# A low-rank factor taken tile by tile instead of two tiles at a time, in a decoder layer in fp32r

## The chip, the cores and the metric

The kernel runs on one core of a Trainium2 chip. The metric is the device time of one execution in microseconds. The kernel before took 524.78 us, the median of 3 runs (523.88 to 526.72).

## The reference, cut to what matters

One decoder layer on 8 sequences of 112 tokens, 1024 features each: self-attention with 16 heads, then cross-attention of each sequence to 375 context rows, then a linear layer with low-rank adapters. Each of the three is added to its input and normalised.

```python
x = layernorm(x + self_attn(x, Wq, Wk, Wv, Wo))     # x: 8 x 112 x 1024
x = layernorm(x + cross_attn(x, ctx))               # ctx: 8 x 375 x 1024
y = x @ weight.T + bias
A = lora_A[adapter_idx]; Bw = lora_B[adapter_idx]   # rank 16, 3 adapters, one per sequence
lo = (x @ A.T) @ Bw.T                               # "first factor", then "second factor"
x = layernorm(x + y + where(use_lora, lo, 0))
```

## The kernel before, in words

Tokens are tiles of 128: 8 x 112 = 896 tokens are 7 tiles. A tile crosses the border of two sequences, so a sequence is spread over at most two tiles. Every product is made in fp32r from a high and a low part of each operand: high by high, high by low and low by high, so three matmuls for each block of 128 features (`part`, L645 and on).

The last third of the kernel, from the end of the self-attention's output product, interleaves two streams on TensorE by a written order:

- the cross-attention of sequence b: `cross_score(b, ...)` (24 matmuls of 376 columns, cut in a first part of 18 and a last of 6), `turn_cprob(b, ...)` (3 transposes of the probabilities into the PSUM bank `CTURN`, bank 6), `cross_mix(b)` (18 matmuls of 512 columns), and `turn_row(b)` (8 transposes of the normalised rows, which give the linear layer its input `act_hi`, `act_lo`);
- the linear layer of tile i, output half n: `ffn(i, n)`, 24 matmuls of 512 columns (8 steps over k, three each), and then two more matmuls that add the adapters' second factor and the bias from `t_both` (`add_low`, L676 to L685).

`t_both` of a tile comes from the first factor. `low_rank` (L776 to L792) makes it for a pair of tiles: in the middle of `ffn(i, 0)` of the pair's second tile, after step k = 2, it issues 16 matmuls of 256 columns (tile 6 is alone: 128 columns) into bank 6, the same bank that `turn_cprob` uses. Then ScalarE copies the lower partitions out (`keep_t_part`, L1081) and VectorE adds them and multiplies by the selection of the adapter, with two writes for each of two segments per tile (`mask_t`, L1511). TensorE needs the result at `add_low`: that of the pair's first tile after step k = 6 of the same `ffn`, that of the second at its end.

So the first half-groups of a pair are finished together. The order on TensorE is: `ffn(0,0)`, `ffn(1,0)` with `low_rank`, `ffn(0,1)`, `ffn(1,1)`, `ffn(2,0)`, `ffn(3,0)` with `low_rank`, and so on, with the pieces of cross-attention between them.

Each engine works its queue in the written order and stops at a wait. ScalarE rounds loaded weights (`round_ff`, `round_cf`, `round_ct`), copies results out of PSUM (`keep_y`) and normalises (`norm_y`, `norm_x2`); VectorE makes the low parts (`rest_cf`, `rest_ct`, `rest_turned`) and statistics (`measure_y`, `add_row`); GpSimd makes the low parts of the linear layer's weights (`rest_ff`, L1757) and the reciprocal roots (`power`, L1741); SyncE issues the DMAs. `ffn` alternates between two PSUM banks, so `wait_bank` lets a group start when the one two before it has been copied out. `GROUPS` lists this order of groups; its index is what `group_done` and `y_kept` count. A ring of `T_RING` = 3 holds `t_both`.

In the functions below these waits matter: `low_rank` waits for `t_rest` (the previous pass has been used up by VectorE) and for `cprob_rest` (the probabilities in bank 6 have been read); `turn_cprob` waits for `t_rest` with its argument `low`.

Of the kernel before, what the change touches and what calls it, by code (L numbers as in the profile page):

```python
# [7 lines left out]
F32 = mybir.dt.float32  # L8
F32R = mybir.dt.float32r
I32 = mybir.dt.int32  # L10
ALU = mybir.AluOpType
# [37 lines left out]
          + [(i, n) for j in range(0, TILES, 2) for n in range(2) for i in range(j, min(j + 2, TILES))])  # L49
# [43 lines left out]


def pair_of(j):

    return range(2 * j, min(2 * j + 2, TILES))


def pair_cols(j):  # L100
    return slice(2 * j * P, min(2 * j + 2, TILES) * P)
# [6 lines left out]
def tile_of(i):  # L108
    return slice(i * P, i * P + P)
# [13 lines left out]
def build(nc, x_feat, x_tok, qkv_w, wo_w, ffn_w, ctx_feat, ctx_tok, starts, rotary, causal,  # L123
          identity, route, out):
    st = ExitStack()
    with st:
        def at(name, shape, where, dt=F32):
            return nc.alloc_sbuf_tensor_at(name, shape, dt, offset=BASE + where)
# [59 lines left out]
        ctop = at("ctop", [S, B, 4], S0 + 32544)  # L188
# [31 lines left out]
        t_part = small("t_part", [RA, 2 * P])  # L220
# [3 lines left out]
        norm = [small("norm1", [P, TILES, 6]), small("norm2", [S, B, 6]), small("norm3", [P, TILES, 6])]  # L224
        assert spot[0] <= 212832, spot
# [87 lines left out]
        def _(sp):  # L313
# [164 lines left out]
            load_cf(19)  # L478
            load_ff(9)
            load_cf(20)  # L480
# [52 lines left out]
        def _(pe):  # L533
# [143 lines left out]
            def add_low(i, n):  # L677

                to = GROUP[group_of(i, n, 1)]
                pe.wait_ge(b_rest, 1)  # L680
                pe.wait_ge(t_rest, 2 * i + 2)
                pe.matmul(to[:, :], t_both[:, i % T_RING, :], b_hi[:, 4 * n:4 * n + 4, :],  # L682
                          start=False, stop=False)
                pe.matmul(to[:, :], t_both[:, i % T_RING, :], b_lo[:, 4 * n:4 * n + 4, :],  # L684
                          start=False, stop=True).then_inc(group_done, 1)  # L685
# [90 lines left out]
            def low_rank(j, turns):  # L776

                cols = pair_cols(j)
                w = cols.stop - cols.start
                pe.wait_ge(a_rest, 1)  # L780
                pe.wait_ge(cprob_rest, turns)
                if j:
                    pe.wait_ge(t_rest, 4 * j)
                for k in range(KT):
                    if k == 0:
                        pe.matmul(CTURN[0:SECOND + RA, 0:w], a_both[:, k, :], act_hi[:, k, cols],
                                  start=True, stop=False)
                    pe.matmul(CTURN[0:SECOND, 0:w], a_both[:, k, 0:SECOND],
                              act_lo[:, k, cols], start=False, stop=False)
                    if k > 0:  # L790
                        last = pe.matmul(CTURN[0:SECOND + RA, 0:w], a_both[:, k, :],
                                         act_hi[:, k, cols], start=False, stop=(k == KT - 1))  # L792
                last.then_inc(t_done, 1)
# [75 lines left out]
            ffn(0, 0)  # L869
# [39 lines left out]
        def _(act):  # L909
# [171 lines left out]
            def keep_t_part(j):  # L1081
                w = P * len(pair_of(j))
                act.wait_ge(t_done, j + 1)
                if j:
                    act.wait_ge(t_added, j)
                act.activation(t_part[:, 0:w], CTURN[SECOND:SECOND + RA, 0:w],
                               ACT.Copy).then_inc(t_part_kept, 1)
# [95 lines left out]
            round_cf(19)  # L1183
            round_ff(9)
            round_cf(20)
            round_cf(21)
            round_ff(10)
            norm_x1(6)
            round_ct(23)
            round_ff(11)  # L1190
            cross_exp(4)
            round_ff(12)
# [9 lines left out]
            round_ct(26)  # L1202
            round_ct(27)
            keep_y(0, 0)
            round_ct(28)
            keep_cprob_t(4)
# [21 lines left out]
            norm_y(1)  # L1228
            round_cf(28)
            round_cf(29)  # L1230
            round_ct(35)
# [3 lines left out]
            keep_t_part(1)  # L1235
            norm_x2(5)
            round_ct(37)
            round_ct(38)
            keep_y(2, 0)
            round_ct(39)  # L1240
            round_ct(40)
            keep_cprob_t(6)
            keep_y(3, 0)
# [5 lines left out]
            norm_y(2)  # L1249
# [19 lines left out]
            norm_y(5)  # L1269
            keep_t_part(3)  # L1270
# [8 lines left out]
        def _(dve):  # L1279
# [231 lines left out]
            def mask_t(j):  # L1511


                w = P * len(pair_of(j))
                dve.wait_ge(t_part_kept, j + 1)
                dve.tensor_tensor(CTURN[0:RA, 0:w], CTURN[0:RA, 0:w], t_part[:, 0:w],
                                  ALU.add).then_inc(t_added, 1)
                dve.wait_ge(low_set, 2)
                dve.wait_ge(t_added, j + 1)
                for i in pair_of(j):  # L1520
                    if i >= T_RING:
                        dve.wait_ge(group_done, group_of(i - T_RING, 1, 1) + 1)
                    at_i = P * (i % 2)
                    for b, _, r, n in segments(i):
                        dve.tensor_scalar(t_both[0:RA, i % T_RING, r:r + n],
                                          CTURN[0:RA, at_i + r:at_i + r + n],
                                          sel[:, b:b + 1], None, ALU.mult).then_inc(t_rounded, 1)
                    for m, (b, _, r, n) in enumerate(segments(i)):
                        dve.wait_ge(t_rounded, 2 * i + m + 1)
                        dve.scalar_tensor_tensor(out=t_both[SECOND:SECOND + RA, i % T_RING, r:r + n],  # L1530
                                                 in0=CTURN[0:RA, at_i + r:at_i + r + n],
                                                 scalar=sel[:, b:b + 1],
                                                 in1=t_both[0:RA, i % T_RING, r:r + n].bitcast(F32),
                                                 op0=ALU.mult, op1=ALU.subtract).then_inc(t_rest, 1)
# [85 lines left out]
            rest_ct(18)  # L1620
            rest_ct(19)
            rest_cprob_t(3)
# [4 lines left out]
            add_wo(13)  # L1627
            rest_cf(19)
# [3 lines left out]
            rest_ct(23)  # L1632
            add_row(3)
            rest_turned("a5")
            rest_cf(22)
            mask_t(0)
            rest_ct(24)
            rest_ct(25)
            rest_ct(26)
            rest_cprob_t(4)  # L1640
            rest_ct(27)
            rest_ct(28)
            measure_y(0, 0)
# [19 lines left out]
            rest_cf(27)  # L1663
            rest_cf(28)
            rest_cf(29)
            cross_top(6)
# [3 lines left out]
            mask_t(1)  # L1670
            rest_ct(36)
            rest_ct(37)
            rest_ct(38)
            rest_ct(39)
            rest_cprob_t(6)
            rest_ct(40)
            measure_y(2, 0)
            measure_y(3, 0)
            rest_turned("b5")
            rest_cf(31)  # L1680
            measure_y(2, 1)
# [8 lines left out]
            rest_ct(46)  # L1690
            measure_y(3, 1)
            rest_turned("b6")
            rest_ct(47)
            add_row(7)
            mask_t(2)
            measure_y(4, 0)
            measure_y(5, 0)
            measure_y(4, 1)
            rest_turned("b7")
            measure_y(5, 1)  # L1700
            mask_t(3)
# [9 lines left out]
        def _(pool):  # L1711
# [90 lines left out]
            rest_ff(8)  # L1802
            rest_ff(9)
            power(0, 6, P)
# [85 lines left out]
```

## Time and profile before

| | |
|---|---|
| median of 3 runs | 524.78 us (523.88 to 526.72) |
| the profiled execution | 525.95 us, of which the span from first to last instruction is 524.2 us |
| TensorE matmuls | busy 515.3 us, 98% of the span, 2868 instructions |
| VectorE / ScalarE / GpSimd | busy 320.3 us (61%) / 261.7 us (50%) / 152.2 us (29%) |
| chain that ended last | TensorE 97%, VectorE 2% |
| granted TensorE clock | 0.997 of full speed, mean over the span |

The page gives the busy time of each engine and, in "the chain that ended last", what each stretch of the span hung on, followed back from the last instruction. A matmul's own duration in the rows (0.39 us for 512 columns) overlaps with its neighbours; what it costs the stream is the distance from its start to the next start. The profiled execution's time is the span and 1.75 us around it.

### The profile page before, as it was taken

What the parts mean: (1) busy time and instruction counts of PE and PEld (TensorE: products, weight loads), DVE (VectorE), ACT (ScalarE), POOL (GpSimd) and SP (SyncE); (2) the same over time, 40 slices, a digit from 0 to 9 for tenths busy, and PEclk for the clock granted to TensorE, in tenths of its full rate; (3) what the DMA queues carried; (4) which work ended last, traced back from release to release, by engine and by line L of the source; (5) the groups of instructions that cost most, each with busy time, mean ns of one, the idle gap of its engine ahead of it and who ended that gap; (6) DMA issues with size and microseconds to landing.
All of it is one profiled execution on the core that took longest, in us unless ns stands there. A gap on an engine that the chain in (4) does not pass through costs nothing.

```text
span 524.2 us, 7773 instructions
## 1 busy us (share of the span) xinstructions
PE 515.3 (98%) x2868; PEld 444.7 (85%) x2868; DVE 320.3 (61%) x660; ACT 261.7 (50%) x663; POOL 152.2 (29%) x139
## 2 busy tenths in 40 slices
PE   8999999999999999999999999999998999999995
PEld 5888888999999999999978888888887888988884
DVE  4832000177776868677674797779987776845432
ACT  5713210173846648384565356357777464525231
POOL 0003600436353554642006250114946010110010
PEclk9999999999999999999999999999999999999998
DMA  9906712331112111100087577579986466433011
GB/s 285 314 16 167 195 40 81 107 136 41 41 48 75 42 40 43 41 1 1 1 257 183 138 207 211 148 198 265 274 243 193 126 194 225 109 87 111 2 75 47
DMA packets 37958, 65.60 MB, mean 125 GB/s; under 512 B 4872, under 2 KB 20616, under 8 KB 37920
## 3 DMA queue, kind: packets, MB, share of 16 engines
q1 hardware_dynamic: 37392, 64.84, 42.9%
q8 instruction: 23, 0.38, 0.3%
q10 hardware_dynamic: 528, 0.26, 0.2%
q14 instruction: 15, 0.12, 0.1%
HBM read 54.08 MB, written 3.67 MB: 110 GB/s over the span
## 4 chain that ended last, share of the span: by engine, by line
PE 97%; DVE 2%; issue 0%; ACT 0%; POOL 0%; POOLq 0%; DVEq 0%
PE bank L536 30%; PE bank L651 29%; PE bank L547 15%; PE bank L737 6%; PE bank L563 3%; PE bank L578 3%; PE bank L770 2%; PE bank L768 2%; PE bank L773 2%; PE bank L721 1%; PE bank L609 1%; PE bank L710 1%; PE bank L682 1%; PE bank L684 1%; DVE cf_lo L1506 1%; PE bank L752 0%
## 5 line engine op out<-in xcount | busy, mean ns | idle before, releaser
L536 PE MATMUL bank<-x_hi,w_hi 128*128 128x448 f32 x256 | 94.3, 368 | 0.0
L536 PE MATMUL bank<-x_hi,w_lo 128*128 128x448 f32 x256 | 93.5, 365 | 0.0
L536 PE MATMUL bank<-x_lo,w_hi 128*128 128x448 f32 x256 | 93.5, 365 | 0.0
L1359 DVE STREAM_TRANSPOSE prob_t<-prob 32x256 f32<-32x256 f32 x160 | 69.7, 436 | 13.0 <-ACT prob L942 10.3
L651 PE MATMUL bank<-wo,act_hi 128*128 128x512 f32 x224 | 70.2, 395 | 0.0
L651 PE MATMUL bank<-ffn,act_hi 128*128 128x512 f32 x224 | 69.9, 393 | 0.0
L1728 POOL TENSOR_TENSOR w_lo<-w_mix,w_hi 128x1024 fp32r<-128x1024 f32 x16 | 38.2, 2389 | 105.2 <-ACT w_hi L917 105.2
L932 ACT ACTIVATE prob<-prob,shift 112x112 f32<-112x112 f32 x128 | 47.8, 375 | 38.9 <-DVE shift L1342 38.9
L1741 POOL TENSOR_TENSOR norm<-norm,minus_half 128x1 f32<-128x1 f32 (+1 forms) x22 | 16.6, 754 | 159.9 <-DVE norm L1432 159.9
L536 PEld LDWEIGHTS bank<-x_hi,w_hi 128*128 128x128 f32 x256 | 48.1, 188 | 4.7
L536 PEld LDWEIGHTS bank<-x_hi,w_lo 128*128 128x128 f32 x256 | 48.1, 188 | 3.8
L536 PEld LDWEIGHTS bank<-x_lo,w_hi 128*128 128x128 f32 x256 | 48.1, 188 | 3.7
L651 PEld LDWEIGHTS bank<-wo,act_hi 128*128 128x128 f32 x224 | 41.3, 188 | 8.7
L651 PEld LDWEIGHTS bank<-ffn,act_hi 128*128 128x128 f32 x224 | 41.2, 188 | 8.1
L1028 ACT ACTIVATE ct_hi<-ct_raw 125x512 fp32r<-125x512 f32 x48 | 28.8, 625 | 33.2 <-DMA ct_raw<-ctx_tok 19.8
L917 ACT ACTIVATE w_hi<-w_mix 128x1024 fp32r<-128x1024 f32 x16 | 16.9, 1054 | 54.8 <-PE bank L536 47.0
L651 PE MATMUL bank<-wo,act_lo 128*128 128x512 f32 x112 | 43.7, 390 | 0.0
L651 PE MATMUL bank<-ffn,act_lo 128*128 128x512 f32 x112 | 43.7, 390 | 0.0
L1506 DVE TENSOR_TENSOR cf_lo<-cf_raw,cf_hi 128x752 fp32r<-128x752 f32 x32 | 34.3, 1081 | 7.8 <-ACT cf_hi L1016 7.6
L942 ACT ACTIVATE prob<-prob,inv 112x112 f32<-112x112 f32 x128 | 37.3, 375 | 0.1
L1322 DVE TENSOR_TENSOR q_feat<-bank,turn 128x448 f32<-128x448 f32 x16 | 9.9, 619 | 43.4 <-PE bank L536 43.3
L1499 DVE TENSOR_TENSOR ct_lo<-ct_raw,ct_hi 125x512 fp32r<-125x512 f32 x48 | 32.9, 719 | 5.4 <-ACT ct_hi L1028 5.1
(114 smaller groups left out, 984.1 us busy)
## 6 DMA issues: line engine op xcount, KB each, us to landing
cf_raw<-ctx_feat SPq DMA_DIRECT2D x32, 376.0 KB, 4.3
ct_raw<-ctx_tok SPq DMA_DIRECT2D x24, 448.0 KB
w_raw<-qkv_w SPq DMA_DIRECT2D x16, 512.0 KB, 3.4
half_raw<-wo_w SPq DMA_DIRECT2D x16, 256.0 KB, 6.0
half_raw<-ffn_w SPq DMA_DIRECT2D x16, 256.0 KB, 6.1
wv_raw<-qkv_w SPq DMA_DIRECT2D x15, 256.0 KB, 7.5
x_raw<-x_feat SPq DMA_DIRECT2D x7, 448.0 KB, 8.2
out<-y_t SPq DMA_DIRECT2D x6, 512.0 KB, 3.6
```

Of the source, the lines that this page charges most:

```text
L536: last = pe.matmul(to[:, 0:HT], a[:, k, :], b[:, k, HT * h:HT * h + HT], start=(k == 0 and b is x_hi and a is w_hi[w]), stop=(k == KT - 1 ...
L547: return pe.matmul(value_bank(c, i)[:, :], a[:, k, tile_of(i)], w[c][:, k, :], start=(k == 0 and a is x_hi and w is wv_hi), stop=(k == KT ...
L651: last = pe.matmul(to[:, :], a[:, k, cols], weight(of, n, k, w), start=(k == 0 and a is act_hi and w == 0), stop=(ends and k == KT - 1 and ...
L737: last = pe.matmul(CSCORE[0:S, 0:LKP], a[:, k, tokens_of(b)], c[slot][:, kk, :], start=(k == 0 and a is act_hi and c is cf_hi), stop=(k == ...
L917: act.activation(w_hi[w][:, :, :], w_mix[:, :, :], ACT.Copy).then_inc(w_rounded, 1)
L932: last = act.activation(prob[a][:, b, :], prob[a][:, b, :], ACT.Exp, bias=shift[:, a, b:b + 1], accum_out=total[:, a, b:b + 1])
L942: last = act.activation(prob[a][:, b, :], prob[a][:, b, :], ACT.Copy, scale=inv[:, a, b:b + 1])
L1028: act.activation(ct_hi[m % CT_HI][:, :], ct_raw[c][:, HALF * n:HALF * n + HALF], ACT.Copy).then_inc(ct_rounded, 1)
L1359: return dve.transpose(quads(prob_t_wide[r], key, query), quads(prob_wide[r], query, key))
L1499: dve.tensor_tensor(ct_lo[c][:, cols], ct_raw[c][:, cols], ct_hi[m % CT_HI][:, :].bitcast(F32), ALU.subtract).then_inc(ct_rest[n], 1)
L1506: dve.tensor_tensor(cf_lo[slot][:, :, :], cf_raw[slot][:, :, :], cf_hi[slot][:, :, :].bitcast(F32), ALU.subtract).then_inc(cf_rest, 1)
L1728: pool.tensor_tensor(w_lo[w][:, :, :], w_mix[:, :, :], w_hi[w][:, :, :].bitcast(F32), ALU.subtract).then_inc(w_rest, 1)
```

## The change

The first factor is made for one tile at a time: `low_rank(i)` issues its 16 matmuls with 128 columns after step k = 2 of every `ffn(i, 0)`, and each half-group is finished by its own two `add_low` matmuls at its end. The four passes (three of 256 columns and one of 128) become seven of 128. `GROUPS` for tiles 2 to 6 becomes (2,0), (2,1), (3,0), (3,1), ...; tiles 0 and 1 keep (0,0), (1,0), (0,1), (1,1). `keep_t_part` and `mask_t` follow it, seven in place of four; `t_part` is half as wide, and `ctop` gets a place of its own. The queues of ScalarE, VectorE, GpSimd and SyncE are written anew around this from the fifth sequence's scores on.

```diff
 GROUPS = (...
-          + [(i, n) for j in range(0, TILES, 2) for n in range(2) for i in range(j, min(j + 2, TILES))])
+          + [(0, 0), (1, 0), (0, 1), (1, 1)]
+          + [(i, n) for i in range(2, TILES) for n in range(2)])
@@ sync
             load_ff(8)
             load_cf(19)
+            load_cf(20)
             load_ff(9)
-            load_cf(20)
...
             load_cf(31)
+            store_y(2)
             load_ct(7, 0)
             load_ct(7, 1)
             load_ct(7, 2)
-            store_y(2)
@@ tensor
             def ffn(i, n, turns=0):
                 ...
                 for k in range(KT):
                     part(1, i, n, k, GROUP[g], ends=False)
-                    if n == 0 and k == 2 and i == pair_of(i // 2)[-1]:
-                        low_rank(i // 2, turns)
-                    if n == 0 and k == 6 and i % 2:
-                        add_low(i - 1, 0)
-                if n or i == pair_of(i // 2)[-1]:
-                    add_low(i, n)
+                    if n == 0 and k == 2:
+                        low_rank(i, turns)
+                pe.wait_ge(b_rest, 1)
+                pe.wait_ge(t_rest, 2 * i + 2)
+                pe.matmul(GROUP[g][:, :], t_both[:, i % T_RING, :], b_hi[...], ...)
+                pe.matmul(GROUP[g][:, :], t_both[:, i % T_RING, :], b_lo[...], ...).then_inc(group_done, 1)
...
-            def low_rank(j, turns):
-                cols = pair_cols(j)
-                w = cols.stop - cols.start
+            def low_rank(i, turns):
+                cols = tile_of(i)
                 pe.wait_ge(a_rest, 1)
+                pe.wait_ge(turn_rest, 2 * AT_TURN[f"b{i + 1}"] + 2)
                 pe.wait_ge(cprob_rest, turns)
-                if j:
-                    pe.wait_ge(t_rest, 4 * j)
+                if i:
+                    pe.wait_ge(t_rest, 2 * i)
                 # the same 16 matmuls, over P columns in place of w
...
-            ffn(0, 0)
+            ffn(0, 0, 4)
...
-            ffn(2, 0)
+            ffn(2, 0, 6)
             cross_score(6, last)
             cross_mix(5)
-            ffn(3, 0, 6)
-            turn_cprob(6, 4)
+            ffn(2, 1)
+            turn_cprob(6, 3)
             cross_score(7, first)
             turn_row(5)
-            ffn(2, 1)
+            ffn(3, 0, 7)
             cross_score(7, last)
             cross_mix(6)
             ffn(3, 1)
             turn_cprob(7, 4)
-            ffn(4, 0)
+            ffn(4, 0, 8)
             turn_row(6)
             cross_mix(7)
+            ffn(4, 1)
             ffn(5, 0, 8)
-            ffn(4, 1)
             turn_row(7)
             ffn(5, 1)
@@ scalar (the places of keep_t_part and keep_y; the rest moves by one or two)
             round_cf(19)
+            keep_t_part(0)
+            round_cf(20)
             round_ff(9)
...
             norm_x1(6)
+            keep_y(0, 0)
             round_ct(23)
...
             round_ff(15)
+            keep_t_part(1)
+            norm_x2(3)
             round_ct(24)
-            keep_t_part(0)
-            norm_x2(3)
...
             norm_y(1)
+            keep_t_part(2)
...
             round_turned("b5")
             round_cf(31)
-            keep_y(2, 1)
+            keep_t_part(3)
+            norm_y(2)
+            keep_y(3, 0)
...
             round_ct(46)
             keep_y(3, 1)
+            keep_t_part(4)
+            keep_y(4, 0)
             round_turned("b6")
             round_ct(47)
             norm_y(3)
-            keep_t_part(2)
             norm_x2(7)
-            keep_y(4, 0)
+            keep_y(4, 1)
+            norm_y(4)
+            keep_t_part(5)
             keep_y(5, 0)
-            keep_y(4, 1)
             round_turned("b7")
-            norm_y(4)
@@ vector (mask_t's places)
             add_wo(13)
+            mask_t(0)
             rest_cf(19)
...
             rest_turned("a5")
+            mask_t(1)
             rest_cf(22)
-            mask_t(0)
...
             rest_cf(27)
+            mask_t(2)
...
             rest_cf(31)
+            mask_t(3)
             measure_y(3, 0)
...
             rest_ct(46)
+            mask_t(4)
             measure_y(3, 1)
...
             measure_y(4, 1)
+            mask_t(5)
             measure_y(5, 0)
@@ gpsimd
             rest_ff(8)
+            power(0, 6, P)
             rest_ff(9)
-            power(0, 6, P)
```

## Rows read from the trace of the kernel before

**Rows 1.** The page: busy time, granted clock in 40 slices, chain that ended last.

```profile
PE 515.3 (98%) x2868; PEld 444.7 (85%) x2868; DVE 320.3 (61%) x660; ACT 261.7 (50%) x663; POOL 152.2 (29%) x139
...
PEclk9999999999999999999999999999999999999998
...
PE 97%; DVE 2%; issue 0%; ACT 0%; POOL 0%; POOLq 0%; DVEq 0%
```

**Rows 2.** Waits of TensorE, 300 us to the end: who, for whom, us, times, longest.

```profile
PE bank L682 <- DVE t_both L1530: 1.5, 1, 1.5
```

**Rows 3.** TensorE in time order, first pair's pass: start, us, line, idle before.

```profile
398.97 0.28 PE L786 MATMUL bank<-act_hi,a_both 128*112 128x256 f32 x1
...
400.85 0.63 PE L651 MATMUL bank<-ffn,act_hi 128*128 128x512 f32 x2
...
402.90 0.62 PE L651 MATMUL bank<-ffn,act_hi 128*128 128x512 f32 x2
...
405.26 0.47 PE L682 MATMUL bank<-b_hi,t_both 128*128 128x512 f32 x1 [1.52 <-DVE t_both L1530]
405.57 0.39 PE L684 MATMUL bank<-b_lo,t_both 128*128 128x512 f32 x1
```

**Rows 4.** VectorE and GpSimd in time order, around that wait.

```profile
399.39 1.28 DVE L1455 TENSOR_TENSOR act_lo<-bank,act_hi 128x512 fp32r<-128x512 f32 x2
400.58 3.12 DVE L1506 TENSOR_TENSOR cf_lo<-cf_raw,cf_hi 128x752 fp32r<-128x752 f32 x1
...
404.65 0.47 DVE L1530 SCALAR_TENSOR_TENSOR t_both<-bank,sel,t_both 48x112 fp32r<-48x112 f32 x2
...
400.36 2.54 POOL L1757 TENSOR_TENSOR ffn<-half_raw,ffn 128x512 fp32r<-128x512 f32 x2
```

**Rows 5.** Line 1506 alone: ns min/median/max of its 32 instructions.

```profile
L1506 DVE TENSOR_TENSOR cf_lo<-cf_raw,cf_hi x32: 927/942/3118, 303.9 to 457.9; 128x752 fp32r<-128x752 f32 x32
```

**Rows 6.** TensorE, the third pair's pass.

```profile
486.11 0.28 PE L786 MATMUL bank<-act_hi,a_both 128*112 128x256 f32 x1
...
487.97 0.62 PE L651 MATMUL bank<-ffn,act_hi 128*128 128x512 f32 x2
```

**Rows 7.** TensorE, the pass of tile 6, 128 columns, and the adding matmul.

```profile
506.95 0.22 PE L786 MATMUL bank<-act_hi,a_both 128*112 128x128 f32 x1
...
508.17 0.68 PE L651 MATMUL bank<-ffn,act_hi 128*128 128x512 f32 x2
...
511.65 0.39 PE L682 MATMUL bank<-b_hi,t_both 128*128 128x512 f32 x1
```

**Rows 8.** ScalarE and VectorE behind the passes of pair 3 and tile 6.

```profile
488.17 0.38 ACT L1086 ACTIVATE t_part<-bank 48x256 f32<-48x256 f32 x1 [5.55 <-PE bank L791]
...
509.13 0.27 ACT L1086 ACTIVATE t_part<-bank 48x128 f32<-48x128 f32 x1
...
510.32 0.47 DVE L1530 SCALAR_TENSOR_TENSOR t_both<-bank,sel,t_both 48x16 fp32r<-48x16 f32 x2
```

**Rows 9.** TensorE, ScalarE and VectorE where tile 0's pass will come.

```profile
385.28 0.71 PE L651 MATMUL bank<-ffn,act_hi 128*128 128x512 f32 x2
...
386.55 0.84 ACT L1016 ACTIVATE cf_hi<-cf_raw 128x752 fp32r<-128x752 f32 x1
...
388.63 3.39 DVE L1506 TENSOR_TENSOR cf_lo<-cf_raw,cf_hi 128x752 fp32r<-128x752 f32 x3
```

**Rows 10.** ScalarE, TensorE, VectorE where tiles 2, 4 and 5 will come.

```profile
435.01 1.25 ACT L1103 ACTIVATE y_t<-y_t,norm 128x1024 f32<-128x1024 f32 x1 [0.28 <-POOL norm L1744]
...
473.59 0.71 PE L651 MATMUL bank<-ffn,act_hi 128*128 128x512 f32 x2
...
474.73 0.50 DVE L1490 TENSOR_TENSOR cprob_lo<-bank,cprob_hi 125x336 fp32r<-125x336 f32 x1
...
498.19 0.93 PE L721 MATMUL bank<-ident,row 112*128 112x112 f32 x8
...
501.13 1.24 ACT L1103 ACTIVATE y_t<-y_t,norm 128x1024 f32<-128x1024 f32 x1 [1.28 <-POOL norm L1744]
```

More of the change, by code:

```diff
@@ L92, in copies_of @@
     return [(b, n) for b in range(B) for n, piece in enumerate(pieces(b)) if piece[0] == i]
[L95 to L101, printed above, removed]
 def tokens_of(b):
@@ L675, in wo @@
                 last.then_inc(group_done, 1)
[L677 to L685, printed above, removed]
             def ffn(i, n, turns=0):
@@ L694, in ffn @@
                     part(1, i, n, k, GROUP[g], ends=False)
-                    if n == 0 and k == 2 and i == pair_of(i // 2)[-1]:
-                        low_rank(i // 2, turns)
-                    if n == 0 and k == 6 and i % 2:
-                        add_low(i - 1, 0)
-                if n or i == pair_of(i // 2)[-1]:
-                    add_low(i, n)
+                    if n == 0 and k == 2:
+                        low_rank(i, turns)
+                pe.wait_ge(b_rest, 1)
+                pe.wait_ge(t_rest, 2 * i + 2)
+                pe.matmul(GROUP[g][:, :], t_both[:, i % T_RING, :], b_hi[:, 4 * n:4 * n + 4, :],
+                          start=False, stop=False)
+                pe.matmul(GROUP[g][:, :], t_both[:, i % T_RING, :], b_lo[:, 4 * n:4 * n + 4, :],
+                          start=False, stop=True).then_inc(group_done, 1)
             def turn_tile(i):
@@ L774, in cross_mix @@
                                   start=False, stop=(c == CC - 1)).then_inc(ct_used, 1)
-            def low_rank(j, turns):
-                cols = pair_cols(j)
-                w = cols.stop - cols.start
+            def low_rank(i, turns):
+                cols = tile_of(i)
                 pe.wait_ge(a_rest, 1)
+                pe.wait_ge(turn_rest, 2 * AT_TURN[f"b{i + 1}"] + 2)
                 pe.wait_ge(cprob_rest, turns)
-                if j:
-                    pe.wait_ge(t_rest, 4 * j)
+                if i:
+                    pe.wait_ge(t_rest, 2 * i)
                 for k in range(KT):
                     if k == 0:
-                        pe.matmul(CTURN[0:SECOND + RA, 0:w], a_both[:, k, :], act_hi[:, k, cols],
+                        pe.matmul(CTURN[0:SECOND + RA, 0:P], a_both[:, k, :], act_hi[:, k, cols],
                                   start=True, stop=False)
-                    pe.matmul(CTURN[0:SECOND, 0:w], a_both[:, k, 0:SECOND],
+                    pe.matmul(CTURN[0:SECOND, 0:P], a_both[:, k, 0:SECOND],
                               act_lo[:, k, cols], start=False, stop=False)
                     if k > 0:
-                        last = pe.matmul(CTURN[0:SECOND + RA, 0:w], a_both[:, k, :],
-                                         act_hi[:, k, cols], start=False, stop=(k == KT - 1))
+                        last = pe.matmul(CTURN[0:SECOND + RA, 0:P], a_both[:, k, :],
+                                         act_hi[:, k, cols],
+                                         start=False, stop=(k == KT - 1))
                 last.then_inc(t_done, 1)
@@ L1079, in round_low, with keep_t_part @@
                 act.activation(b_hi[:, :, :], b_raw[:, :, :], ACT.Copy).then_inc(b_rounded, 1)
[L1081 to L1086, printed above, removed]
+            def keep_t_part(i):
+                act.wait_ge(t_done, i + 1)
+                if i:
+                    act.wait_ge(t_added, i)
+                act.activation(t_part[:, :], CTURN[SECOND:SECOND + RA, 0:P],
                                ACT.Copy).then_inc(t_part_kept, 1)
@@ L1234, in _ @@
             round_ct(36)
-            keep_t_part(1)
             norm_x2(5)
             round_ct(37)
+            keep_cprob_t(6)
             round_ct(38)
-            keep_y(2, 0)
             round_ct(39)
             round_ct(40)
-            keep_cprob_t(6)
-            keep_y(3, 0)
+            keep_y(2, 1)
             round_turned("b5")
             round_cf(31)
-            keep_y(2, 1)
+            keep_t_part(3)
+            norm_y(2)
+            keep_y(3, 0)
             round_ct(41)
             cross_exp(7)
-            norm_y(2)
             round_ct(42)
@@ L1260, in _ @@
             norm_y(3)
-            keep_t_part(2)
             norm_x2(7)
-            keep_y(4, 0)
+            keep_y(4, 1)
+            norm_y(4)
+            keep_t_part(5)
             keep_y(5, 0)
-            keep_y(4, 1)
             round_turned("b7")
-            norm_y(4)
             keep_y(5, 1)
             norm_y(5)
-            keep_t_part(3)
+            keep_t_part(6)
             keep_y(6, 0)
@@ L1508, in rest_cf, with mask_t @@
                                   ALU.subtract).then_inc(cf_rest, 1)
[L1511 to L1516, printed above, removed]
+            def mask_t(i):
+                dve.wait_ge(t_part_kept, i + 1)
+                dve.tensor_tensor(CTURN[0:RA, 0:P], CTURN[0:RA, 0:P], t_part[:, :],
                                   ALU.add).then_inc(t_added, 1)
@@ L1518, in mask_t @@
                 dve.wait_ge(low_set, 2)
[L1519 to L1534, printed above, removed]
+                if i >= T_RING:
+                    dve.wait_ge(group_done, group_of(i - T_RING, 1, 1) + 1)
@@ new lines, in mask_t @@
+                dve.wait_ge(t_added, i + 1)
+                for b, _, r, n in segments(i):
+                    dve.tensor_scalar(t_both[0:RA, i % T_RING, r:r + n], CTURN[0:RA, r:r + n],
+                                      sel[:, b:b + 1], None, ALU.mult).then_inc(t_rounded, 1)
+                for m, (b, _, r, n) in enumerate(segments(i)):
+                    dve.wait_ge(t_rounded, 2 * i + m + 1)
+                    dve.scalar_tensor_tensor(out=t_both[SECOND:SECOND + RA, i % T_RING, r:r + n],
+                                             in0=CTURN[0:RA, r:r + n], scalar=sel[:, b:b + 1],
+                                             in1=t_both[0:RA, i % T_RING, r:r + n].bitcast(F32),
+                                             op0=ALU.mult, op1=ALU.subtract).then_inc(t_rest, 1)
@@ L1620, in _ @@
             rest_ct(18)
+            rest_cprob_t(3)
             rest_ct(19)
-            rest_cprob_t(3)
             rest_ct(20)
@@ L1669, in _ @@
             rest_cf(30)
-            mask_t(1)
             rest_ct(36)
             rest_ct(37)
+            rest_cprob_t(6)
             rest_ct(38)
             rest_ct(39)
-            rest_cprob_t(6)
             rest_ct(40)
-            measure_y(2, 0)
+            rest_turned("b5")
+            measure_y(2, 1)
+            rest_cf(31)
+            mask_t(3)
             measure_y(3, 0)
-            rest_turned("b5")
-            rest_cf(31)
-            measure_y(2, 1)
             cross_top(7)
@@ L1694, in _ @@
             add_row(7)
-            mask_t(2)
-            measure_y(4, 0)
+            measure_y(4, 1)
+            mask_t(5)
             measure_y(5, 0)
-            measure_y(4, 1)
             rest_turned("b7")
             measure_y(5, 1)
-            mask_t(3)
+            mask_t(6)
             measure_y(6, 0)
```

17 lines of the change are left out of this document (9 added, 8 removed).

## The prediction

> **What bounds the kernel now.** I read the page's busy times, its clock row and its chain first. TensorE's matmuls fill 98% of the span, its clock is at the higher of its two levels in every slice but a last one, and 97% of the chain that ended last is TensorE [rows 1]. So the time is the length of TensorE's stream plus the holes in it. Next come TensorE's waits: over the last 224 us there is one, for `t_both`, 1.5 us [rows 2]. Every other engine's work is under cover there. I therefore price two things, the length of what TensorE issues and the holes, and for the reordered queues I only ask whether they open a hole. Last I read TensorE in time order around the passes of `low_rank`, and the other engines beside the hole.
>
> **The passes get dearer.** A pass of 256 columns takes 400.85 - 398.97 = 1.88 us, and the third 487.97 - 486.11 = 1.86 [rows 3, 6]; the second shows the same, so 1.87 each, 117 ns for each of 16 matmuls. A pass of 128 columns takes 508.17 - 506.95 = 1.22 us, 76 ns each [rows 7]: half the columns cost 65%. A step over k of `ffn` is (402.90 - 400.85) / 3 = 0.683 us [rows 3]; behind the pass of 128 columns, five steps take 511.65 - 508.17 = 3.48 in place of 3.42, so I charge that pass 0.06 more: 1.28. Tile 6 has its pass already. Three pairs' passes go, 3 x 1.87 = 5.61, and six single ones come, 6 x 1.28 = 7.68: **+2.07 us**, all on TensorE and thus on the path, +0.69 for each pair. Bounds: if a single pass costs half of a pair's (0.94), the sum is +0.03; if it is charged the 117 ns of the wide matmul, 1.87 each, it is +5.6. I take the row of the same instruction with the same columns, 1.28, which is the nearest there could be.
>
> The Trainium skill bears on this ("TensorE: Matmul & The Clock Gate", Back-to-back issue gap): it gives an isolated matmul of 128 columns about 56 ns. By that a pass would be 0.9 us and the passes no dearer than before; the row's 76 ns speaks against it. The same section's figure for a stream with weight loads, about 81 ns, is close to the row.
>
> The other instructions on TensorE stay: 14 pairs of adding matmuls, the same `ffn` matmuls, the same transposes, with the same kinds of neighbours. Splitting the passes also doubles `keep_t_part` and `mask_t` on ScalarE and VectorE; they have idle time, priced below as slack.
>
> **The hole closes.** `add_low(0,0)` could have started at 402.90 + 0.68 = 403.58 and started at 405.26, and the next matmul came 0.31 behind it where the usual distance is 0.23: the hole costs 1.68 + 0.08 = **1.76 us** [rows 3]. Its cause: `mask_t(0)` stands on VectorE behind `rest_cf(22)`, which took 3.12 us (median of its line 0.94) because GpSimd ran two `rest_ff` at 400.36 to 402.90 [rows 4, 5]. In the new order `mask_t(0)` runs 14 us earlier, and `mask_t(1)` stands ahead of `rest_cf(22)`. I take the whole 1.76 as gone. If it stayed, the sum is dearer by 1.76; more than this hole cannot be gained, since there is no other.
>
> What stalled can be read in the trace: an instruction with both inputs in SBUF beside GpSimd's reading ones; the subtraction of `act_lo`, one input in PSUM, kept its usual 0.64 us each until 400.58 [rows 4]. The Trainium skill says the same as a rule ("SBUF — State Buffer", Who interferes with whom): such a pair blocks, a VectorE instruction with at most one SBUF input does not. `mask_t`'s reads are of that kind, so by the rule `mask_t(1)` would pass GpSimd's last two `rest_ff`, which now come at the same time; if the rule failed there, a wait of up to 1 us returns.
>
> **Is a new hole opened?** After its own pass a tile's `t_both` is now needed five steps later, 3.48 us [rows 7]. At the least it takes 0.20 us until ScalarE starts (488.17 - 487.97) and 510.32 + 0.47 - 509.13 = 1.66 from there to the last write [rows 6, 8]: 1.86, which leaves 1.6 us for whatever is ahead in the two queues.
> - Tile 0: pass at 385.28 + 2.14 = 387.42 to 388.64 [rows 9]. ScalarE has finished `round_cf(19)` at 387.4 and VectorE `add_wo(13)` at 388.6 [rows 9]: slack 1.6. Behind `mask_t(0)` waits `rest_cf(19)`, done about 391.5; `cross_score(4, last)` needs it at 392.6. GpSimd's `rest_ff(9)` can hold it 1.2 us longer: 0 to 0.2 us of wait.
> - Tile 1: TensorE is 1.28 + 0.46 = 1.74 late here, pass ends about 401.9; VectorE is through `rest_turned(a5)` at 400.58 + 1.74 = 402.3 [rows 4], so `t_both` comes about 404.0 against a need at 405.4: slack 1.4.
> - Tile 2: `norm_y(1)` is ahead on ScalarE and ended at 436.26 [rows 10]; the pass will end about 435.5, so ScalarE is up to 0.8 late: slack 0.9. Tile 3 has `rest_cf(31)` ahead on VectorE, which follows the same `turn_row` as the pass does: about the same.
> - Tile 4: ahead are the last three `round_ct` and `rest_ct`, done about when the pass ends: slack about 1.2. This pass has a new wait of its own: bank 6 must be free of the probabilities of sequence 7. They were read at 474.73 + 0.50 = 475.23, and the pass would be reached at 473.59 + 2.15 = 475.74 [rows 10]: slack 0.5, the thinnest. What waits behind it on TensorE is everything.
> - Tile 5: `norm_y(4)` is ahead. It starts 501.13 - 498.19 = 2.94 after its group's end and takes 1.24 [rows 10], 4.2 in all; the pass ends 2.1 + 1.2 = 3.3 after it. So ScalarE is 0.9 late and the slack 0.7 to 0.9.
>
> None reaches zero. SyncE's two moves (`load_cf(20)` before `load_ff(9)`, `store_y(2)` before three loads) and `power(0, 6)` before `rest_ff(9)` on GpSimd: what they overtake is needed many us later (`store_y(2)` waits for `norm_y(2)`, which ScalarE now does before `cross_mix(6)` starts, and the loads wait for that product anyway). Zero, with 0 to 0.5 as bounds. The bank waits (`y_kept`) follow the group two before, which ended over 6 us earlier. The tail after the last product is untouched.
>
> **Sum.** +2.07 - 1.76 = +0.3 us. On the profiled execution's own terms the span goes 524.2 to 524.5 and its time 525.95 to 526.3. The median of the runs, 524.78, is 1.2 below the profiled execution; I put the difference on it: **525.1 us**.
>
> **The rivals.**
> - *One hole is left or a new one of its size comes* (the slack of 0.5 at tile 4, `rest_cf(19)` at tile 0): +2.07 - 1.76 + 1.7 = +2.0, 526.8. For it: four places under 1 us. Against: the work ahead in the queues shifts with TensorE itself.
> - *The hole was that execution's own.* The profiled one is 1.2 slower than the median, and the hole comes of GpSimd taking its turn 0.2 us before VectorE. If the timed runs have none, the change only costs: 526.9. Against: that turn follows from VectorE's own statistics, in each run alike.
> - *The other side: `t_both` late at every tile.* Each group now ends on its own pass, with nothing of the other tile between. The first pair's chain took 405.12 - 400.85 = 4.3 us from the pass [rows 3, 4]. If each of six new passes has such a chain, each costs 4.3 - 3.48 + 0.2 = 1.0, and with no hole gone elsewhere: +2.07 - 1.76 + 6.0 = +6.3, 531.1. It decides from a chain of 3.48 us on. Two of before speak against it: tile 6's was done at 510.79, 2.6 us after its pass, though ScalarE came 0.96 late to it, and pair 3's ScalarE started 0.2 behind its pass [rows 6 to 8].
> - *Cheap passes.* At half the pair's price the sum is +0.03 - 1.76 = -1.7, 523.1.
> - *The change doesn't do what it says:* no sign, the passes are plainly seven.
>
> **Chances.** Forecast 60%; a hole left or new 14%; the hole not in the timed runs 12%; late at every tile, in part or whole, 8%; cheap passes 6%. A measurement of this kernel tells about 0.5% from no change, 2.6 us, so only the chain late at most tiles is slower by more, with a little of the two middle cases, and hardly anything is faster. Faster 3%, same 87%, slower 10%. Range 523.1 to 527.5: from cheap passes to a new hole with some delay beside it; above lies the rest of the late chains. The forecast's own range is 524.3 to 526.1.
>
> **What would show it.** Seven passes of some 1.2 us, none of 256 columns; no wait at L682's counterpart, or one of tenths; the span's matmul count up by 48; `rest_cf(22)` may still be long, behind `mask_t(1)`. From the last `turn_row` to the end TensorE's order is the same, so the shift must be complete there: +0.3. The step from the first pair alone should be 2 x 1.28 - 1.87 - 1.76 = -1.1, then +0.7 for each of two pairs. I am wrong if waits for `t_both` or for bank 6 appear, or if single passes cost other than 1.2 to 1.35.

## The result, and the profile after

The changed kernel took 526.49 us, the median of 22 runs (525.85 to 527.56), against 525.07 us for the kernel before in 22 runs (523.69 to 526.72). The ratio is 1.0029, 95% interval 1.0021 to 1.0037: slower by 1.1 to 1.9 us. The two medians lie 1.42 apart, the ratio says +1.5. Forecast were +0.3 us and 525.1 us. The time lies in the stated range (523.1 to 527.5), but outside the forecast's own (524.3 to 526.1), and the shift is several times the forecast's.

The page of the changed kernel, its lines on busy time, granted clock and the chain that ended last, as in [rows 1]:

```profile
PE 516.7 (98%) x2916; PEld 446.8 (85%) x2916; DVE 318.5 (61%) x663; ACT 262.2 (50%) x666; POOL 152.0 (29%) x139
...
PEclk9999999999999999999999999999999999999999
...
PE 98%; ACT 1%; DVE 0%; issue 0%; POOL 0%; POOLq 0%; ACTq 0%
```

TensorE has 48 matmuls more, as counted, and bounds the kernel as before. Its waits from 300 us on (who, for whom, us, times, longest) answer to [rows 2]:

```profile
PE bank L751 <- DVE ct_lo L1485: 0.6, 1, 0.6
```

The wait for `t_both` is gone and another has come. TensorE in time order shows where: `turn_row(2)`, the pass of tile 0 and what follows it, its adding matmul, the wait inside `cross_mix(3)`, `turn_cprob(4)`, and `turn_row(7)`.

```profile
383.90 0.93 PE L704 MATMUL bank<-ident,row 112*128 112x112 f32 x8
...
386.74 0.22 PE L769 MATMUL bank<-act_hi,a_both 128*112 128x128 f32 x1
...
387.96 0.68 PE L643 MATMUL bank<-ffn,act_hi 128*128 128x512 f32 x2
...
391.44 0.39 PE L680 MATMUL bank<-b_hi,t_both 128*128 128x512 f32 x1
...
396.17 0.39 PE L756 MATMUL bank<-ct_hi,cprob_lo 125*112 125x512 f32 x1
397.14 0.49 PE L751 MATMUL bank<-ct_hi,cprob_hi 125*112 125x512 f32 x1 [0.58 <-DVE ct_lo L1485]
...
406.03 0.48 PE L735 MATMUL bank<-ident,cprob 112*125 112x112 f32 x3
...
498.73 0.45 PE L704 MATMUL bank<-ident,row 112*128 112x112 f32 x3
```

The pass takes 387.96 - 386.74 = 1.22 us, as read from tile 6 [rows 7]. The wait costs 397.14 - 396.17 - 0.23 = 0.74 us, and about 0.1 behind it.

The two spans, 524.2 and 524.7, differ by 0.5 only, and that is misleading. `turn_row(2)`, ahead of everything that the change touches, starts at 383.90 here and at 384.58 before. The lead is there already at the first query projection (first start in the window, the last column but one: 82.9 us before, 82.2 after):

```profile
L528 PE MATMUL bank<-x_hi,w_hi x30: 362/366/370, 82.2 to 99.8; 128*128 128x448 f32 x30
```

So I compare stretches between fixed marks of TensorE's stream, in us. The stretch "first" goes from `turn_row(2)` to `turn_cprob(4)` and holds the first two passes and both places of waits; "middle" goes on to `turn_row(7)`; "end" to the end of the span.

| execution | `turn_row(2)` starts | first | middle | end |
|---|---|---|---|---|
| before, shown above | 384.58 | 22.37 | 91.24 | 26.0 |
| before, e9 / e10 / e11 | 385.00 / 385.22 / 385.23 | 21.26 / 20.67 / 21.40 | 91.24 / 91.24 / 91.22 | 26.0 each |
| changed, shown here | 383.90 | 22.13 | 92.70 | 26.0 |
| changed, e1 / e12 | 385.05 / 384.94 | 21.33 / 21.63 | 92.69 / 92.72 | 25.9 / 26.0 |
| e3, e4, e5 (before, altered) | 385.08 / 385.33 / 384.85 | 21.54 / 20.59 / 20.82 | 91.22 / 91.24 / 91.21 | 26.0 / 25.9 / 26.0 |
| e2, e6 (changed, altered) | 384.95 / 384.31 | 21.50 / 21.50 | 92.72 / 92.72 | 25.9 / 26.0 |

Middle and end repeat within 0.1 us; the start varies by 1.4 us and "first" by 1.8. The middle is 1.46 longer in the changed kernel, for two pairs of tiles. In what follows, the loss of an execution in "first" is what it takes over the shortest of its kind: 20.59 in e4 for the kernel before, 21.33 in e1 for the changed one, the two with no stop of TensorE in their traces.

### The profile page after: what moved, and what is told of

It is laid out like the page before. It is cut to its first block, busy times and chain, and to the rows that moved or that the text cites. A ratio compares the mean times of both kernels' runs of the same rounds, so it can differ in the third digit from the quotient of the medians.

```text
span 524.7 us, 7890 instructions
## 1 busy us (share of the span) xinstructions
PE 516.7 (98%) x2916; PEld 446.8 (85%) x2916; DVE 318.5 (61%) x663; ACT 262.2 (50%) x666; POOL 152.0 (29%) x139
## 4 chain that ended last, share of the span: by engine, by line
PE 98%; ACT 1%; DVE 0%; issue 0%; POOL 0%; POOLq 0%; ACTq 0%
PE bank L528 30%; PE bank L643 29%; PE bank L539 15%; PE bank L720 6%; PE bank L555 3%; PE bank L570 3%; PE bank L751 2%; PE bank L753 2%; PE bank L756 2%; PE bank L704 1%; PE bank L693 1%; PE bank L774 1%; PE bank L601 1%; PE bank L771 1%; PE bank L682 1%; PE bank L680 1%
## 5 line engine op out<-in xcount | busy, mean ns | idle before, releaser
L1012 ACT ACTIVATE ct_hi<-ct_raw 125x512 fp32r<-125x512 f32 x48 | 28.5, 623 | 35.0 <-DMA ct_raw<-ctx_tok 23.0
L539 PE MATMUL bank<-wv_hi,x_hi 128*128 128x512 f32 x112 | 36.2, 393 | 0.0
```

Of the source, the lines that this page charges most:

```text
L539: return pe.matmul(value_bank(c, i)[:, :], a[:, k, tile_of(i)], w[c][:, k, :], start=(k == 0 and a is x_hi and w is wv_hi), stop=(k == KT ...
L1012: act.activation(ct_hi[m % CT_HI][:, :], ct_raw[c][:, HALF * n:HALF * n + HALF], ACT.Copy).then_inc(ct_rounded, 1)
```

## The experiments

**e1: the changed kernel again.** No edit.

> The changed kernel unaltered, for comparison on the same chip. Theory: in the stretch that the change touches (from the start of ffn(0,0)) TensorE's passes cost +2.07 us, the old hole of 1.76 is gone, and a new hole of 0.8 us stands in cross_mix(3), where its last chunk of context waits for its low part: sum +1.1 to +1.4 against the kernel before, ratio about 1.0025, with the new hole in the trace at the same place. Rival (the old hole was not in the timed runs of before): the ratio is above that, 1.0045 or so, since the gain of 1.76 would be missing.

Measured: 527.16 us against 525.35, ratio 1.0038 (1.0022 to 1.0054), that is +2.0 us (1.2 to 2.8), between the theory and the rival. The wait in `cross_mix(3)` is not there in its trace. ScalarE in time order shows why the place is shaky: two roundings of weights, one of context features and `round_ct(23)` (L1012):

```profile
390.87 0.63 ACT L1054 ACTIVATE ffn<-half_raw 128x512 fp32r<-128x512 f32 x1 [0.56 <-DMA half_raw<-ffn_w]
392.50 0.83 ACT L1000 ACTIVATE cf_hi<-cf_raw 128x752 fp32r<-128x752 f32 x1 [0.99 <-DMA cf_raw<-ctx_feat]
393.64 0.63 ACT L1054 ACTIVATE ffn<-half_raw 128x512 fp32r<-128x512 f32 x1 [0.31 <-DMA half_raw<-ffn_w]
...
395.93 0.62 ACT L1012 ACTIVATE ct_hi<-ct_raw 125x512 fp32r<-125x512 f32 x1
```

The same of the first profile of the changed kernel, with `norm_x1(6)` (L1017) and `keep_y(0,0)` (L1081):

```profile
390.61 0.63 ACT L1054 ACTIVATE ffn<-half_raw 128x512 fp32r<-128x512 f32 x1 [1.45 <-DMA half_raw<-ffn_w]
392.20 0.84 ACT L1000 ACTIVATE cf_hi<-cf_raw 128x752 fp32r<-128x752 f32 x1 [0.96 <-DMA cf_raw<-ctx_feat]
393.36 0.63 ACT L1054 ACTIVATE ffn<-half_raw 128x512 fp32r<-128x512 f32 x1 [0.33 <-DMA half_raw<-ffn_w]
393.90 1.23 ACT L1017 ACTIVATE x_t<-x_t,norm 128x1024 f32<-128x1024 f32 x1
395.15 0.60 ACT L1081 ACTIVATE y_t<-bank 128x512 f32<-128x512 f32 x1
395.65 0.62 ACT L1012 ACTIVATE ct_hi<-ct_raw 125x512 fp32r<-125x512 f32 x1
```

TensorE is 1.15 us later in e1 (385.05 against 383.90), but the loads land only 0.28 later (393.64 against 393.36). ScalarE takes them in order, so `round_ct(23)` follows the loads' clock, and TensorE waits for it if it is early. In this stretch the DMA engines are full; the last three numbers of this row of the changed kernel's windows (granted clock, DMA share, GB/s) say so:

```profile
390.00:395.00 5.00, 5.00 (x25) 4.12 (x24) 4.90 (x9) 3.11 (x4) 2.60 (x4) 1.00 1.04 263
```

Between these two executions a lead from the kernel's start is partly handed back here.

**e2: the changed kernel, SyncE's swap undone.**

```diff
-            load_cf(20)
             load_ff(9)
+            load_cf(20)
```

> The changed kernel with SyncE's queue as before at one place: load_ff(9) ahead of load_cf(20) again. Theory A (the new hole comes of this swap: the weight block lands late, ScalarE stands at round_ff(9), so norm_x1(6), keep_y(0,0) and round_ct(23) run late): the hole in cross_mix(3) goes, 0.8 us less than the changed kernel, +0.3 to +0.6 against before; round_ff(9) starts by 389.9. Theory B (the hole comes of the order on ScalarE alone, keep_y(0,0) ahead of round_ct(23)): the hole keeps its size within 0.2 us.

Measured: 526.79, ratio 1.0027 (1.0014 to 1.0040). No wait in `cross_mix(3)`, but e1 had none either, so this trace cannot tell A from B. `round_ff(9)` started at 390.12 with no wait in front, in e1 at 390.87, and `round_ct(23)` at 395.41, in e1 at 395.93, with TensorE 0.1 us apart. That looks like the price of the swap, but e12 below, the changed kernel with the swap in it and TensorE at the same point, has the times of e2:

```profile
390.11 0.62 ACT L1054 ACTIVATE ffn<-half_raw 128x512 fp32r<-128x512 f32 x1
...
395.42 0.62 ACT L1012 ACTIVATE ct_hi<-ct_raw 125x512 fp32r<-125x512 f32 x1
```

So that half microsecond is a difference between two executions, and no run shows that the swap costs anything. In the timed runs the intervals of e1 and e2 overlap. The trace of e2 loses 0.17 us at another place, `cross_score(4, last)`.

**e3: the kernel before, `mask_t(0)` first.**

```diff
-            rest_cf(22)
             mask_t(0)
+            rest_cf(22)
```

> The kernel before with mask_t(0) ahead of rest_cf(22) on VectorE, nothing else. Theory (the hole of 1.76 us at the first adding matmul is real in each run, and comes of mask_t(0) standing behind rest_cf(22)): the hole is gone, -1.7 us, ratio 0.9967. Rival (the hole was that one execution's own): no change in the timed runs, within 0.4 us. If keep_t_part came too late as well, some tenths of the hole would stay.

Measured: 525.09 against 525.35, ratio 0.9987 (0.9972 to 1.0002): the 1.76 us are not there to be gained. In its trace 0.58 us of wait is left, 0.8 with what it costs around it, and now for another reason. TensorE, ScalarE and VectorE in time order:

```profile
404.93 0.47 PE L682 MATMUL bank<-b_hi,t_both 128*128 128x512 f32 x1 [0.58 <-DVE t_both L1530]
...
402.21 0.63 ACT L1028 ACTIVATE ct_hi<-ct_raw 125x512 fp32r<-125x512 f32 x1 [0.20 <-DMA ct_raw<-ctx_tok]
402.87 0.38 ACT L1086 ACTIVATE t_part<-bank 48x256 f32<-48x256 f32 x1
...
403.28 0.42 DVE L1516 TENSOR_TENSOR bank<-bank,t_part 48x256 f32<-48x256 f32 x1 [1.96 <-ACT t_part L1086]
```

`keep_t_part(0)` stood behind a rounding that waited for its load, and started at 402.87; in the first trace it started at 401.05, and TensorE's pass lay 0.65 us earlier there.

**e4: the kernel before, GpSimd's `power(1, 3)` later.**

```diff
-            power(1, 3, S)
             rest_ff(14)
             rest_ff(15)
+            power(1, 3, S)
```

> The kernel before with GpSimd's power(1,3) moved behind rest_ff(14) and rest_ff(15), nothing else. Theory (rest_cf(22) took 3.12 in place of 0.94 us because GpSimd's two rest_ff held the reading port in front of it): GpSimd now has them done by about 401.7 at the latest or interleaves them earlier, rest_cf(22) takes 0.9 to 2.0 us, and the hole of 1.76 shrinks to 0 to 0.5: -1.3 to -1.8 us. Rival (rest_cf(22) was slow for another reason, such as the DMA traffic of that moment): it stays near 3.1 us and the time stays within 0.4 us of before.

Measured: 525.06 against 525.35, ratio 0.9995 (0.9980 to 1.0010), span of the profile 523.1. TensorE's adding matmul comes without a wait; `rest_cf(22)` takes 1.10 in place of 3.12 us [rows 4], in between GpSimd's `rest_ff`:

```profile
404.33 0.39 PE L682 MATMUL bank<-b_hi,t_both 128*128 128x512 f32 x1
...
401.33 1.10 DVE L1506 TENSOR_TENSOR cf_lo<-cf_raw,cf_hi 128x752 fp32r<-128x752 f32 x1
...
399.07 4.51 POOL L1757 TENSOR_TENSOR ffn<-half_raw,ffn 128x512 fp32r<-128x512 f32 x3
```

"First" is 20.59, against 22.37: 1.78 less, the whole hole. So the mechanism read from the first trace fits that execution; the timed runs say that it is not what a run usually pays. The trace of e4 alone does not test it: in e9 to e11 below, without the edit, `rest_cf(22)` takes 0.93.

**e5 and e6: both kernels cleaned of their waits.** e5 is the kernel before with both edits above and `keep_t_part(0)` ahead of `round_ct(24)`; e6 the changed one with

```diff
-            load_cf(20)
             load_ff(9)
+            load_cf(20)
...
-            keep_y(0, 0)
             round_ct(23)
+            keep_y(0, 0)
```

> The kernel before with everything ahead of the first pair's t_both taken away that can be: mask_t(0) ahead of rest_cf(22), keep_t_part(0) ahead of round_ct(24), power(1,3) behind rest_ff(15). Theory (the hole of before comes and goes with the landing of loads, and cost less than 1 us in the mean of the timed runs): its trace has no hole, 20.6 us from the third turn_row to the fifth turn_cprob, and the timed runs gain 0.3 to 1.0 us. Rival (the hole is in every run at 1.76): -1.8 us.

> The changed kernel without its new hole: load_ff(9) ahead of load_cf(20), and round_ct(23) ahead of keep_y(0,0) on ScalarE. Theory: no hole in cross_mix(3); the stretch takes 21.3 to 21.5 us, and against the cleaned kernel before the timed runs lie +2.0 to +2.3 us higher, which is the price of the passes alone; against before +1.2 to +1.8. Rival (something else than passes and holes makes the changed kernel slower, such as a longer tail or the clock): more than 2.6 us over the cleaned before.

Measured: e5 524.42 against 524.63, ratio 0.9995 (0.9984 to 1.0006), so what its edits take away costs at most 0.8 us in the mean of the timed runs. e6 526.50, ratio 1.0040 (1.0025 to 1.0056). Between the two medians lie 2.08 us (the means of 6 and 12 runs are 2.3 apart, 1.7 to 3.0); the passes alone are 2.19 by the traces. No third cause is needed.

The traces are not quite as clean as expected. e6 has no wait in `cross_mix(3)`, but loses 0.17 us at `cross_score(4, last)`. e5 has none for `t_both`, but loses 0.23 at the last chunk in `cross_mix(3)`, the very place where the changed kernel waited, though it has neither the swap nor `keep_y(0, 0)` there. The unaltered kernel before loses 0.16 there in e11. TensorE's first matmul on that chunk, in e5 and then in e11, comes 0.39 and 0.30 us behind the one ahead of it in place of 0.23:

```profile
395.75 0.49 PE L768 MATMUL bank<-ct_hi,cprob_hi 125*112 125x512 f32 x1
```

```profile
396.03 0.49 PE L768 MATMUL bank<-ct_hi,cprob_hi 125*112 125x512 f32 x1
```

Neither cleaned kernel is measurably faster than its original, and none of the versions beats the kernel before beyond its interval.

**e7 and e8: every pass twice.** In `low_rank`, `for _ in range(2):` around the loop over k, in the changed kernel and in the one before.

> The changed kernel with each of its seven passes of low_rank issued twice (the second starts the sum anew, the output is the same). Theory (a pass of 128 columns costs the stream 1.22 us, and about 0.06 behind it): +8.5 to +9.0 us over the changed kernel, 10.0 to 10.6 over before. If a pass cost half a pair's, +6.6; if the full pair's, +13.

> The kernel before with each of its four passes issued twice. Theory (1.87 us for 256 columns, 1.22 for 128): +6.8 us over before. A hole may grow or shrink by some tenths, since t_both of the first pair is then 1.87 us later in the stream of TensorE, but so is its use.

Measured: e7 535.39 against 524.63, ratio 1.0203 (1.0186 to 1.0220), and e8 531.01, ratio 1.0120 (1.0104 to 1.0136): +10.7 (9.8 to 11.5) and +6.3 (5.5 to 7.1), both as expected within their intervals. By the marks, "middle" grew to 97.77 with four passes more, (97.77 - 92.70) / 4 = 1.27 us each; and to 94.98 in the kernel before with two more, (94.98 - 91.24) / 2 = 1.87. Half the columns cost 68%.

**e9 to e12: more executions of the unaltered kernels.** No edit: e9 to e11 are the kernel before, e12 the changed one.

> The kernel before unaltered, one more profiled execution. Theory (its hole comes and goes with GpSimd's turn at the reading port and the landing of loads): the stretch from the third turn_row to the fifth turn_cprob takes between 20.6 and 22.4 us, and what it takes over 20.6 stands in the trace as a wait for t_both, with rest_cf(22) longer than 0.94 us. Rival (the hole is fixed, 1.76 in each execution): 22.3 to 22.4.

> As the look before it, a third profiled execution of the kernel before: the theory expects the three to differ by more than 0.5 us in this stretch and to agree within 0.1 in all others behind it; the rival expects 22.3 to 22.4 again.

> A fourth profiled execution of the kernel before. Over the four the theory expects a mean hole of 0.3 to 1.0 us; the rival 1.76.

> The changed kernel unaltered, a third profiled execution. Theory: 21.3 us from the third turn_row to the fifth turn_cprob and 0 to 0.9 for a wait in cross_mix(3), the larger the earlier TensorE reaches the stretch; 92.7 us from there to the last turn_row, as in the two others.

Four executions of the kernel before spend 22.37, 21.26, 20.67 and 21.40 us in "first": over the 20.60 of a clean one that is 1.77, 0.66, 0.07 and 0.80, mean 0.8. At the adding matmul itself stand 1.76, 0.5, 0 and 0.6 of it, mean 0.7. The rest is 0.1 to 0.2 at `cross_score(4, last)` in e9 and e10 and 0.16 in `cross_mix(3)` in e11, the two places where the changed kernel loses too.

In all three new executions VectorE's `rest_cf(22)` took 0.93 us: the 3.12 of the first trace is in none of them. What is left of the hole in e9 and e11 comes of ScalarE, where `keep_t_part(0)` started at 402.51 and 402.88, in e10 at 401.90, behind roundings of loads. In e9, VectorE came first and GpSimd waited: `rest_cf(22)` (L1506) took its 0.93 us, and two `rest_ff` took 3.14 in place of 2.54. `keep_t_part(0)` was late from ScalarE:

```profile
401.15 0.93 DVE L1506 TENSOR_TENSOR cf_lo<-cf_raw,cf_hi 128x752 fp32r<-128x752 f32 x1
402.92 0.42 DVE L1516 TENSOR_TENSOR bank<-bank,t_part 48x256 f32<-48x256 f32 x1 [0.84 <-ACT t_part L1086]
...
401.34 3.14 POOL L1757 TENSOR_TENSOR ffn<-half_raw,ffn 128x512 fp32r<-128x512 f32 x2 [0.34 <-ACT ffn L1070]
...
404.57 0.47 PE L682 MATMUL bank<-b_hi,t_both 128*128 128x512 f32 x1 [0.26 <-DVE t_both L1530]
```

In e10 both were in time:

```profile
401.31 0.93 DVE L1506 TENSOR_TENSOR cf_lo<-cf_raw,cf_hi 128x752 fp32r<-128x752 f32 x1
...
404.31 0.39 PE L682 MATMUL bank<-b_hi,t_both 128*128 128x512 f32 x1
```

e12, the changed kernel, has its loss (0.30) at a third place, `cross_score(4, last)`, the one foreseen with 0 to 0.2: `rest_cf(19)` behind `rest_ff(9)`. TensorE leaves a gap from 392.71 + 0.23 to 393.17; GpSimd had started 0.45 us ahead of VectorE:

```profile
392.71 0.39 PE L682 MATMUL bank<-b_lo,t_both 128*128 128x512 f32 x1
393.17 0.40 PE L720 MATMUL bank<-cf_hi,act_hi 128*112 128x376 f32 x1
...
391.38 3.35 DVE L1492 TENSOR_TENSOR cf_lo<-cf_raw,cf_hi 128x752 fp32r<-128x752 f32 x3
...
390.93 1.30 POOL L1741 TENSOR_TENSOR ffn<-half_raw,ffn 128x512 fp32r<-128x512 f32 x1
```

A second wait at the same line in `cross_mix(3)`, 0.45 us, is in e7, which reached `turn_row(2)` at 384.01, nearly as early as the first trace of the changed kernel. It is no second case of e1's account. The high part of the chunk was rounded at 396.07 there, but VectorE's `rest_ct(23)` started at 396.87 and took 1.63 us in place of 0.69, beside two `rest_ff` of GpSimd:

```profile
396.87 1.63 DVE L1486 TENSOR_TENSOR ct_lo<-ct_raw,ct_hi 125x512 fp32r<-125x512 f32 x1
...
396.67 2.98 POOL L1742 TENSOR_TENSOR ffn<-half_raw,ffn 128x512 fp32r<-128x512 f32 x2 [1.16 <-ACT ffn L1055]
```

So the account of e1, an early TensorE and loads that land when they land, rests on one execution.

## Why the prediction held, and the step that failed

- **TensorE bounds the kernel, the time is its stream plus its holes.** Right: middle and end repeat within 0.1 us from one execution of a kernel to the next, and what varies in "first" stands in the traces as stops of TensorE.
- **The passes, +2.07.** Right. The clean stretches differ by 21.33 - 20.60 = 0.73 in "first" and 1.46 in "middle": +2.19 us. A narrow pass is 1.27 with what follows it (charged: 1.28), a wide one 1.87. The Trainium skill's figure for an isolated matmul of 128 columns ("TensorE: Matmul & The Clock Gate", Back-to-back issue gap; about 56 ns), by which the passes would have come out free, does not hold in this stream: e7 prices the doubled passes at 1.27 us, 79 ns for a matmul.
- **The hole closes, -1.76.** This is the step that failed. "I take the whole 1.76 as gone" took one execution's hole for that of every run. It was the largest of four, and the mean is 0.8. The cause was right for that execution only: the rival that the hole was its own had 12% and was argued away with "that turn follows from VectorE's own statistics, in each run alike", and e9, e10 and e11 all show the turn the other way round, with 0.93 us for `rest_cf(22)`. The sign that was there: that execution took 525.95 us, 1.2 more than the median.
- **No new hole, 0 to 0.5.** The queue slacks at the six new passes held. Tile 5, the one with the least room for `t_both`, shows how they are read: ScalarE's `norm_y(4)` and `keep_t_part(5)`, VectorE's last write, TensorE's use.

```profile
494.47 1.24 ACT L1086 ACTIVATE y_t<-y_t,norm 128x1024 f32<-128x1024 f32 x1 [2.15 <-POOL norm L1728]
495.74 0.27 ACT L1069 ACTIVATE t_part<-bank 48x128 f32<-48x128 f32 x1
...
496.98 0.47 DVE L1512 SCALAR_TENSOR_TENSOR t_both<-bank,sel,t_both 48x32 fp32r<-48x32 f32 x2
...
498.27 0.39 PE L680 MATMUL bank<-b_hi,t_both 128*128 128x512 f32 x1
```

  `t_both` is done at 497.45, 0.8 ahead of its use, as worked out (0.7 to 0.9). The list of slacks has no line for `cross_mix(3)`, though: SyncE's swap was passed with "what they overtake is needed many us later", and `keep_y(0, 0)` ahead of `round_ct(23)` was not priced. TensorE comes 1.76 us later there, and yet one execution of three lost 0.8 us; another lost 0.3 at `cross_score(4, last)`; the mean is 0.4. Neither place is new: the kernel before loses 0.1 to 0.2 at one or the other in three of its four executions. By the rows `keep_y(0, 0)` holds `round_ct(23)` up by 0.50 us; what the swap adds no run shows.
- **The sum.** With measured sizes: +2.19 - 0.8 + 0.4 = +1.8, against +1.5 (1.1 to 1.9) in the 22 runs and +2.0 (1.2 to 2.8) in e1's. The means of the losses are over four and three executions and are good to some tenths only. The first pair's step, forecast at -1.1, is +0.3 between these means. Both middle rivals, a new hole and a hole that the timed runs lack, came true in part. Late `t_both` at every tile and cheap passes are refuted.
- **How much of it was luck.** The range spans 4.4 us and holds both middle rivals (526.8 and 526.9), and 526.49 lies nearer to them than to 525.1. The price of the passes and the slacks of `t_both` were forecast well; that the time came out in the range says little about the rest.

What stays open: what made the wait in `cross_mix(3)` of the first trace. Its place can lose 0.2 us without the swap and without `keep_y(0, 0)` (e5, e11), no run takes `keep_y(0, 0)` alone out of the way, and e2, with the swap undone, reached the place too late to wait with it or without. Also open is why the loads land when they do: the rounding in front of `norm_x1(6)`, which waits for its load in each of the four executions of the kernel before, started anywhere from 391.26 to 392.96.

## What to carry to other kernels

A hole read from one profile is a draw, not a price: compare that execution's time with the median, and take two or three more profiles before a gain is booked on it. In this stream half the columns cost 68% (117 ns for a matmul of 256 columns, 79 for one of 128), so cutting a pass in two is a cost on a kernel that TensorE bounds, and the latency it saves must be one that is paid in every run. A difference between one trace with an edit and one without is no price either: e1 and e2 differed by 0.5 us at the instruction in question, and e12, a second trace without the edit, took that away. When queues are written anew, list the slack behind every instruction that waits for a load, and not only behind the ones that the change is about.

## What the runs showed of the hardware

- Two inputs in SBUF on VectorE and a reading GpSimd instruction exclude each other, and whoever starts first wins: VectorE 3.12 in place of 0.94 us behind two of GpSimd's in a row [rows 4], GpSimd 3.14 in place of 2.54 in e9, where VectorE had started 0.19 us ahead. The Trainium skill has it so ("SBUF — State Buffer", Who interferes with whom), and the traces agree. `mask_t` beside GpSimd's `rest_ff`, in the changed kernel, kept its usual durations:

```profile
402.67 0.29 DVE L1501 TENSOR_TENSOR bank<-bank,t_part 48x128 f32<-48x128 f32 x1
403.42 0.47 DVE L1508 TENSOR_SCALAR t_both<-bank,sel 48x96 fp32r<-48x96 f32 x2 [0.46 <-DVE bank L1501]
403.92 0.47 DVE L1512 SCALAR_TENSOR_TENSOR t_both<-bank,sel,t_both 48x96 fp32r<-48x96 f32 x2
...
402.73 2.55 POOL L1741 TENSOR_TENSOR ffn<-half_raw,ffn 128x512 fp32r<-128x512 f32 x2
```

  The pause of 0.46 us ahead of the second instruction is in all six traces of the changed kernel and its variants at this tile, and 0.1 at tiles 0 and 5 and in e3, where `mask_t(0)` runs beside the same kind of GpSimd work; no run explains it.
- TensorE reaches `turn_row(2)` anywhere from 383.9 to 385.3 us, ahead of all that the change touches on TensorE. That is about half of the 3.0 us between the shortest and the longest timed run of the kernel before.
